# Block attention: 64-row head operands with shift and mask rows, filled by DMA, and an even first-pass stream

## The chip, the cores and the metric

The kernel runs on one core of one Trainium2 chip. The metric is the device time of one execution in microseconds (us), lower is better. Three timed executions of the kernel before gave 1613.99, 1619.00 and 1619.61 us, so the median is 1619.0 us.

## The reference, cut to what matters

Four blocks follow each other on `x` of shape (2, 1024, 128): rotary attention, a mixture of 8 experts, block attention and a channel mix. Only the third is touched. It has 16 heads of 8 channels and this core:

```python
q = (hidden_states @ Wq.T + bq).reshape(B, S, NUM_HEADS, HEAD_DIM)
k = (hidden_states @ Wk.T + bk).reshape(B, S, NUM_HEADS, HEAD_DIM)
v = (hidden_states @ Wv.T + bv).reshape(B, S, NUM_HEADS, HEAD_DIM)
scores = jnp.einsum('bihd,bjhd->bhij', q, k) / scale
blk = jnp.arange(S) // WINDOW                  # WINDOW = 32
allowed = blk[:, None] >= blk[None, :]
scores = jnp.where(allowed, scores, jnp.zeros((), scores.dtype))
probs = jax.nn.softmax(scores, axis=-1)
ctx = jnp.einsum('bhij,bjhd->bihd', probs, v).reshape(B, S, H)
return ctx @ Wo.T + bo
```

A score that is not allowed is 0, not minus infinity, so later keys still count in the softmax, each with weight exp(0 - maximum).

## The kernel before

`block_attention` first projects `q` and `k` (the part that ends in lines 1000 to 1032). Each head gets 32 rows of `q_all` and of `k_all`: its 8 channels four times over, split in high and low parts for fp32r matmuls. Then the main part works on 8 groups (2 batches times 4 groups of 4 heads), each in two passes.

The first pass finds the maximum of each query's row. A fill step `i` of a group does two heads (`query_scores`, lines 1160 to 1178): a matmul with 32 rows of queries as weights and up to 512 keys moving (L1173), and a matmul with 3 mask rows (L1176) on the 128x128 block on the diagonal. The result lies in one of three PSUM banks `score_ps`, and VectorE takes its maximum (`row_max`, L1300) and frees the bank. A group has 20 fill steps, listed in `KINDS`, that is 40 banks. From the maxima VectorE makes rows of shifts, TensorE transposes them (`shift_transposes`, L1129, L1130) and ScalarE keeps them in `shift` and `later` (L1258, L1259).

The second pass goes by key tiles of 128 keys. A group has 24 steps: `block_of` gives the half of the queries, the key tile `kt` and the pair of heads `hp`. `key_scores` (L1140) multiplies keys (weights) by up to 512 queries for two heads, `key_shifts` (L1151, L1156) adds shift and mask rows in matmuls of 5 or 2 rows over the same columns, and ScalarE takes the exponential of both heads into `probs_T` (`exps`, L1268). After every second step `values` (L1190) multiplies 9 columns of `v_den` by `probs_T` for four heads; for the key tiles 0 to 3 of either half it adds the later keys (`suffix`, L1196). `keep_out` (L1274) copies the sum, `turn` (L1206) transposes it, `divide` (L1327, L1332) finishes it. After the last group of a batch come `transpose_attn` (L1214), `project` (L1222) and the additions to the residual.

The order is written out by hand: for `m` in 0 to 9 and `i` in 0 to 23 the step `(m, i)` runs the second pass of group `m - 1` and, for `i` below 20, a fill step of group `m`. The heads of the two lie in different row quarters of TensorE. The program order in a step is `key_scores`, `query_scores(i, 0)`, `key_shifts`, `query_scores(i, 1)`, and then `values` if `i` is odd:

```python
def fill_of(i, x):
    return KINDS[i // 2], 2 * (1 - i % 2) + x
...
pe.wait_ge(bank_free, n - 2)      # query_scores: one of three banks must be free
```

`m = 0` has only fill steps, `m = 8` only the second pass of the last group. SyncE issues nothing in the main part. GpSimd clears `zeros` there; in the projection part it clears and copies constants from `fixed` (lines 919 to 937), and VectorE waits for that (`zeroed`, 2) before line 1032.

Of the kernel before, what the change touches and what calls it, by code (L numbers as in the profile page):

```python
# [10 lines left out]
P = 128  # L11
B, N, D = 2, 1024, 128
T = B * N // P
TB = N // P
# [8 lines left out]
HG = 4  # L23
EPS = 1e-5
NEVER = 2.0 ** 99
BLOCK_CONSTS = 1307
# [829 lines left out]
def block_attention(nc, core, consts, Wq, bq, Wk, bk, Wv, bv, Wo, bo):  # L856
# [6 lines left out]
    with ExitStack() as st:  # L863
# [6 lines left out]
        shift_keys = sb("shift_keys", [P, P], F32R)  # L870
        mask_q, mask_k = sb("mask_q", [P, P], F32R), sb("mask_k", [P, P], F32R)
        fixed = sb("fixed", [P, BLOCK_CONSTS])
        later_cap = fixed[:, 776:792].rearrange("p (t h) -> p t h", t=4)
        own_block = fixed[:, 792:920].rearrange("p (i t r) -> p i t r", i=2, t=4)
        shift_rows = [sb(f"shift_rows{i}", [P, 4, HG, 32]) for i in range(2)]
# [3 lines left out]
        with ExitStack() as st2:  # L879
# [37 lines left out]
            with nc.Block() as block:  # L917
                @block.gpsimd
                def _(pool):
# [9 lines left out]
                    for i in range(2):  # L929
                        below = fixed[:, 920:923].rearrange("p (t h r) -> p t h r", t=1, h=1).broadcast_to([P, 4, HG, 3])  # L930
                        nc.gpsimd.tensor_copy(shift_rows[i][:, :, :, 2:5], below)
# [3 lines left out]
                    nc.gpsimd.tensor_copy(shift_keys[:], fixed[:, 923:1051])  # L935
                    nc.gpsimd.tensor_copy(mask_q[:], fixed[:, 1051:1179])
                    nc.gpsimd.tensor_copy(mask_k[:], fixed[:, 1179:1307]).then_inc(zeroed, 1)
# [98 lines left out]
        STEPS = 24  # L1036
        KINDS = ((0, 0, 1), (1, 0, 2), (2, 0, 3), (3, 0, 4), (4, 0, 4), (5, 0, 4), (6, 0, 4), (6, 4, 7), (7, 0, 4), (7, 4, 8))
        FILL_STEPS = 2 * len(KINDS)
        Z_STEP, T_HALF0, T_HALF1 = 9, 16, 4
        TURN0, TURN1, KEEP0, KEEP1 = 13, 4, 11, 2  # L1040
        shift = [sb(f"shift{i}", [P, N], F32R) for i in range(2)]
        later = [sb(f"later{i}", [P, 2, P]) for i in range(2)]
        lowest = sb("lowest", [P, 12, HG])
        capped = sb("capped", [P, 4, HG])
        probs_T = [sb(f"probs_T{i}", [P, HG, 512]) for i in range(3)]
        out_kept = [sb(f"out_kept{i}", [P, 512]) for i in range(2)]
        rden = [sb(f"rden{i}", [P, 4, HG]) for i in range(2)]
        attn = sb("attn", [P, TB, H1, DH1])
# [5 lines left out]
        out_ps = ps("out", [P, 512])  # L1054
        bank_filled, bank_free = sem("bank_filled"), sem("bank_free")
        pair_filled, pair_free = sem("pair_filled"), sem("pair_free")
        capped_ready, halves_ready, shift_ready = sem("capped_ready"), sem("halves_ready"), sem("shift_ready")
        pv_done, out_copied, rden_ready, main_cleared = (sem(n) for n in ("pv_done", "out_copied", "rden_ready", "main_cleared"))

        def filling(m, i):  # L1060

            return m < GROUPS and i < FILL_STEPS

        def summing(m):

            return 1 <= m <= GROUPS

        def turned(m, i):

            if i == TURN0 and 1 <= m <= GROUPS:  # L1070
                return m - 1, 0
            if i == TURN1 and 2 <= m <= GROUPS + 1:
                return m - 2, 1
            return None

        def projected(m, i, after):

            got = turned(m, i - after)
            return got if got and got[0] % G == G - 1 else None

        bank, pair = {}, {}
        for m in range(GROUPS + 2):
            for i in range(STEPS):
                if (i == T_HALF1 and summing(m)) or (i == T_HALF0 and m < GROUPS):
                    pair["shift", m, i] = len(pair)
                if summing(m):
                    pair["scores", m, i] = len(pair)
                if filling(m, i):
                    for x in range(2):
                        bank["fill", m, i, x] = len(bank)  # L1090
                if turned(m, i):
                    bank["turn", m, i] = len(bank)
                if projected(m, i, 3):
                    bank["attn_T", m, i] = len(bank)
                if projected(m, i, 6):
                    bank["project", m, i] = len(bank)

        def fill_of(i, x):

            return KINDS[i // 2], 2 * (1 - i % 2) + x  # L1100

        def block_of(i):

            half, r = (0, i) if i < 8 else (1, i - 8)
            return half, r // 2, r % 2
# [5 lines left out]
        def keyed(m):  # L1111

            return (m - 1) * 12

        with nc.Block() as block:
            @block.gpsimd
            def _(pool):
                nc.gpsimd.memset(zeros[:], 0.0).then_inc(main_cleared, 1)

            @block.tensor  # L1120
            def _(pe):
                def shift_transposes(half, m, i):
                    n = pair["shift", m, i]
                    if n >= 2:
                        pe.wait_ge(pair_free, n - 1)
                    pe.wait_ge(halves_ready, 2 * (m - half) + half + 1)
# [5 lines left out]
                def key_scores(m, i):  # L1132
                    half, kt, hp = block_of(i)
                    b, g = (m - 1) // G, (m - 1) % G
                    lo, hi = columns(half, kt)
                    n = pair["scores", m, i]
                    pe.wait_ge(pair_free, max(n - 1, pair["shift", m if half else m - 1, T_HALF1 if half else T_HALF0] + 1))
                    for x in range(2):
                        rows = slice(64 * hp + 32 * x, 64 * hp + 32 * x + 32)
                        nc.tensor.matmul(score_T_ps[n % 2][:, x, 0:hi - lo], k_all[rows, g, b * N + kt * P:b * N + kt * P + P],  # L1140
                                         q_all[rows, g, b * N + lo:b * N + hi], start=True, stop=False)

                def key_shifts(m, i):
                    half, kt, hp = block_of(i)
                    lo, hi = columns(half, kt)
                    n = pair["scores", m, i]
                    off = P if lo == P * kt else 0
                    if off:
                        for x in range(2):
                            rows = slice(64 * hp + 32 * x, 64 * hp + 32 * x + 5)  # L1150
                            ins = nc.tensor.matmul(score_T_ps[n % 2][:, x, 0:P], shift_keys[rows, :], shift[(m - 1) % 2][rows, lo:lo + P],  # L1151
                                                   start=False, stop=hi - lo == P)
                    if hi - lo > off:
                        for x in range(2):
                            rows = slice(64 * hp + 32 * x, 64 * hp + 32 * x + 2)
                            ins = nc.tensor.matmul(score_T_ps[n % 2][:, x, off:hi - lo], shift_keys[rows, :], shift[(m - 1) % 2][rows, lo + off:hi],  # L1156
                                                   start=False, stop=True)
                    ins.then_inc(pair_filled, 1)

                def query_scores(m, i, x):  # L1160
                    (t, lo, hi), h = fill_of(i, x)
                    b, g = m // G, m % G
                    n = bank["fill", m, i, x]
# [5 lines left out]
                    rows = slice(32 * h, 32 * h + 32)  # L1169
                    for t, lo, hi, at in parts:  # L1170
                        width = (hi - lo) * P
                        own = hi == t + 1
                        ins = nc.tensor.matmul(score_ps[n % 3][:, at:at + width], q_all[rows, g, b * N + t * P:b * N + t * P + P],  # L1173
# [382 lines left out]
```

## Time and profile before

| | us |
|---|---|
| median of three timed executions | 1619.0 |
| the profiled execution, its own time | 1619.23 |
| its span, first to last instruction | 1617.3 |
| main part of block attention in it, first to last fill or second-pass step | 1171.1 to 1575.7 |

The profiled execution is an ordinary one: its time lies within those of the timed three. Times in rows are from the start of the span. "PE" is TensorE's matmuls, "PEld" its weight loads, "DVE" VectorE, "ACT" ScalarE, "POOL" GpSimd, "SP" SyncE. PEclk is the clock that TensorE was granted, as a share of 2.4 GHz; it has two levels, 1.0 and 0.5 (1.2 GHz), and a value between is a mean of the two over the stretch. In a timeline row the first number is the start, the second how long the merged run of instructions took, and `x8` how many they are; a release by another engine stands in brackets.

### The profile page before, as it was taken

What the parts mean: (1) busy time and instruction counts of PE and PEld (TensorE: products, weight loads), DVE (VectorE), ACT (ScalarE), POOL (GpSimd) and SP (SyncE); (2) the same over time, 40 slices, a digit from 0 to 9 for tenths busy, and PEclk for the clock granted to TensorE, in tenths of its full rate; (3) what the DMA queues carried; (4) which work ended last, traced back from release to release, by engine and by line L of the source; (5) the groups of instructions that cost most, each with busy time, mean ns of one, the idle gap of its engine ahead of it and who ended that gap; (6) DMA issues with size and microseconds to landing.
All of it is one profiled execution on the core that took longest, in us unless ns stands there. A gap on an engine that the chain in (4) does not pass through costs nothing. (4 is left out here: it accounts for less than half of the span.)

```text
span 1617.3 us, 26411 instructions
## 1 busy us (share of the span) xinstructions
PE 1429.3 (88%) x9399; PEld 967.4 (60%) x9400; DVE 830.4 (51%) x1461; ACT 892.0 (55%) x1582; POOL 280.9 (17%) x206
## 2 busy tenths in 40 slices
PE   3499999999999999999999962954899999999995
PEld 2377777777777777777777741642465455555443
DVE  5355445555555555555545532535775564464406
ACT  2277777777777777777777720311624444353443
POOL 3233113312321232123212303023000000000000
PEclk9799999999999999999999975985955565585557
DMA  4542344234423442344234423111000000000001
GB/s 129 127 111 73 78 110 110 71 78 110 110 69 75 109 116 56 82 110 117 59 83 110 111 90 126 45 46 40 1 1 1 1 1 1 1 1 1 1 1 31
DMA packets 53477, 104.93 MB, mean 65 GB/s; under 512 B 9010, under 2 KB 30004, under 8 KB 53300
## 3 DMA queue, kind: packets, MB, share of 16 engines
q1 hardware_dynamic: 52004, 100.59, 25.2%
q0 software_dynamic: 1424, 3.67, 0.8%
q8 instruction: 32, 0.52, 0.1%
q14 instruction: 17, 0.14, 0.0%
HBM read 18.70 MB, written 5.31 MB: 15 GB/s over the span
## 5 line engine op out<-in xcount | busy, mean ns | idle before, releaser
L507 DVE TENSOR_REDUCE a_negmax<-a_score 128x1 f32<-128x1024 f32 x257 | 314.5, 1224 | 327.4 <-PE a_score L371 327.4
L468 ACT ACTIVATE a_probs_T<-a_tr 128x512 f32<-128x512 f32 x514 | 279.2, 597 | 214.4 <-PE a_tr L377 210.9
L474 ACT ACTIVATE a_probs<-a_score,a_negmax 128x1024 f32<-128x1024 f32 x256 | 287.9, 1124 | 28.6 <-DVE a_negmax L507 28.5
L377 PE MATMUL a_tr<-ident,a_probs 128*128 128x128 f32 x2056 | 267.2, 273 | 0.4 <-ACT a_probs_T L468 0.4
L377 PEld LDWEIGHTS a_tr<-ident,a_probs 128*128 128x128 f32 x2056 | 239.5, 140 | 38.0 <-issue 5.7
L432 PE MATMUL a_out<-a_probs_T,a_v 128*64 128x256 f32 x2096 | 255.1, 385 | 0.0
L1300 DVE TENSOR_REDUCE a_lowest<-a_score 128x1 f32<-128x512 f32 (+3 forms) x320 | 183.8, 630 | 131.8 <-PE a_score L1176 81.1
L1268 ACT ACTIVATE a_probs_T<-a_score_T 128x1024 f32<-128x1024 f32 (+1 forms) x192 | 149.0, 809 | 171.5 <-PE a_score_T L1156 150.8
L432 PEld LDWEIGHTS a_out<-a_probs_T,a_v 128*64 128x64 f32 x2096 | 138.8, 136 | 96.8 <-issue 38.0
L1173 PE MATMUL a_score<-a_k_all,a_q_all 32*128 32x512 f32 (+3 forms) x384 | 164.3, 611 | 5.3 <-DVE a_lowest L1300 5.0
L331 POOL TENSOR_TENSOR a_rden<-a_rden_col,a_ones 128x256 f32<-128x256 f32 x65 | 68.4, 1052 | 557.3 <-DVE a_rden_col L530 557.3
L1190 PE MATMUL a_out<-a_probs_T,a_v_den 128*9 128x512 f32 (+3 forms) x768 | 132.2, 779 | 4.5 <-ACT a_out_kept L1274 4.3
L1140 PE MATMUL a_score_T<-a_q_all,a_k_all 32*128 32x512 f32 (+3 forms) x384 | 114.4, 614 | 0.8 <-ACT a_probs_T L1268 0.6
L1173 PEld LDWEIGHTS a_score<-a_k_all,a_q_all 32*128 32x128 f32 x384 | 85.1, 276 | 28.8 <-DVE a_lowest L1300 23.9
L1156 PE MATMUL a_score_T<-a_shift,a_shift_keys 2*128 2x512 f32 (+3 forms) x320 | 85.2, 530 | 0.0
L371 PE MATMUL a_score<-a_k_stack0ah,a_q_stack0a 128*128 128x512 f32 x130 | 58.8, 452 | 28.5 <-DMA a_k_stack0bl<-a_k_lo 28.5
L1140 PEld LDWEIGHTS a_score_T<-a_q_all,a_k_all 32*128 32x128 f32 x384 | 56.9, 277 | 39.3 <-ACT a_probs_T L1268 19.3
L1196 PEld LDWEIGHTS a_out<-a_later,a_suffix 16*128 16x128 f32 x128 | 30.0, 289 | 82.6 <-issue 82.6
L523 DVE TENSOR_TENSOR a_attn_T<-a_out,a_rden_b 128x256 f32<-128x256 f32 x66 | 28.0, 424 | 86.9 <-PE a_out L432 86.9
L147 PE MATMUL n_tp<-ident,n_xn 128*128 128x128 f32 x48 | 12.1, 422 | 64.0 <-DVE n_xn L134 64.0
L357 PE MATMUL a_misc<-a_xn_cur,a_w_cur 128*128 128x512 f32 x128 | 65.5, 594 | 0.0
L371 PE MATMUL a_score<-a_k_stack1ah,a_q_stack1a 128*128 128x512 f32 x128 | 57.4, 448 | 6.7 <-DMA a_k_stack1bl<-a_k_lo 6.7
(235 smaller groups left out, 2203.8 us busy)
## 6 DMA issues: line engine op xcount, KB each, us to landing
a_q_rot<-a_q_raw SPq DMA_DIRECT2D x68, 128.0 KB, 2.3
a_k_rot<-a_k_raw SPq DMA_DIRECT2D x68, 128.0 KB, 2.3
a_xn_cur<-normed_T SPq DMA_DIRECT2D x17, 512.0 KB, 3.2
a_k_stack0ah<-a_k_hi SPq DMA_DIRECT2D x18, 256.0 KB, 3.3
a_k_stack0al<-a_k_lo SPq DMA_DIRECT2D x18, 256.0 KB, 4.7
a_k_stack0bh<-a_k_hi SPq DMA_DIRECT2D x18, 256.0 KB, 5.0
a_k_stack0bl<-a_k_lo SPq DMA_DIRECT2D x18, 256.0 KB, 4.7
a_k_stack1ah<-a_k_hi SPq DMA_DIRECT2D x16, 256.0 KB, 3.3
```

Source lines behind the costliest of these rows:

```text
L371: last = nc.tensor.matmul(score_ps[s % 2][:, cols], q_stack[par][h][:, tile * P:tile * P + P], k_stack[par][h][part][:, cols], start=part ...
L377: last = nc.tensor.transpose(tr_ps[k // 4][:, k % 4 * P:k % 4 * P + P], probs[s % 4][:, k * P:k * P + P], core.ident[:])
L432: ins = nc.tensor.matmul(out_ps[64 * h:64 * h + 64, 0:256], v[par if s >= 5 else 1 - par][:, k, 64 * h:64 * h + 64], probs_T[grp][:, h, k, ...
L468: nc.scalar.activation(probs_T[(s - 1) // 4 % 2][:, h, 4 * i:4 * i + 4, tile % 2 * P:tile % 2 * P + P], tr_ps[i][:].rearrange("p (k q) -> ...
L474: nc.scalar.activation(probs[s % 4][:], score_ps[s % 2][:], ACT.Exp, bias=negmax[:, s:s + 1], accum_out=den[:, s:s + 1]).then_inc(probs_re ...
L507: nc.vector.tensor_reduce(negmax[:, s:s + 1], score_ps[s % 2][:], axis=AX.X, op=ALU.max, negate=True)\
L1140: nc.tensor.matmul(score_T_ps[n % 2][:, x, 0:hi - lo], k_all[rows, g, b * N + kt * P:b * N + kt * P + P], q_all[rows, g, b * N + lo:b * N ...
L1156: ins = nc.tensor.matmul(score_T_ps[n % 2][:, x, off:hi - lo], shift_keys[rows, :], shift[(m - 1) % 2][rows, lo + off:hi], start=False, st ...
L1173: ins = nc.tensor.matmul(score_ps[n % 3][:, at:at + width], q_all[rows, g, b * N + t * P:b * N + t * P + P], k_all[rows, g, b * N + lo * P ...
L1190: ins = nc.tensor.matmul(out_ps[32 * h:32 * h + DH1 + 1, lo - 512 * half:512], v_den[:, b, kt, g * HG + h, :], probs_T[n % 3][:, h, 0:hi - ...
L1268: nc.scalar.activation(probs_T[k % 3][:, 2 * hp:2 * hp + 2, 0:hi - lo], score_T_ps[n % 2][:, :, 0:hi - lo], ACT.Exp).then_inc(pair_free, 1)
L1300: nc.vector.tensor_reduce(to, src, axis=AX.X, op=ALU.max, negate=True).then_inc(bank_free, 1)
```

## The change

Each head of a group gets 64 rows of its own in new operands: `q_still` (queries as weights, first pass), `q_moving` (queries moving, second pass) and `k_cur` (keys, both passes). Rows 0 to 31 are the head's rows of `q_all` or `k_all`, rows 32 and 33 the two parts of the shift (ones in `k_cur`), rows 34 to 36 the mask. The mask rows and ones are laid out once by GpSimd, in 14 copies of 128x1024 in the projection part, where three copies of 128x128 and two of 128x48 go. The head's rows come by DMA on SP's queue, 4 copies of 128 KB each for `q_still`, `q_moving` and `k_cur` and for every group; the shift rows come by 4 small DMAs for each half group (`place_shift`).

With this a block of the second pass is one matmul pass of 34 rows (37 on the diagonal) in place of a pass of 32 and one of 2 or 5 rows, and a block of the first pass needs no mask matmul of its own. Two heads now fill the 128 rows, where four row quarters were used.

The loop runs over `j` from -1: `j = -1` does 25 fill steps (`LEAD`), then every step of the second pass is followed by 20/24 of a fill step, until all 160 are done; the last 30 steps have none. The fill step that falls out is that of every sixth step (`j % 6 == 0`). Shift transposes stand ahead of fill step 12 of a group and 4 of the next. `out_kept` and `attn` lie in the space of `core.xT`, and `lowest` has two buffers.

```diff
+        STEPS, FILLS = 24, 20
+        LEAD, LAG = 25, 5
+        TURN0, TURN1, KEEP0, KEEP1 = 13, 28, 10, 26
...
+        def fills_by(j):
+
+            return min(GROUPS * FILLS + LAG, LEAD + (j + 1) * FILLS // STEPS)
+
+        def fills_at(j):
+
+            return range(0, LEAD) if j < 0 else range(fills_by(j - 1), fills_by(j))
...
+                def place_shift(m, half):
+                    sp.wait_ge(shift_kept, 2 * m + half + 1)
+                    for h in range(HG):
+                        sp.dma_start(q_moving[m % 2][h // 2][64 * (h % 2) + 32:64 * (h % 2) + 34, 512 * half:512 * half + 512].bitcast(F32),
+                                     shift[half][32 * h:32 * h + 2, :].bitcast(F32)).then_inc(shift_loaded[half], 16)
+
+                load_still(0)
+                load_keys(0)
+                load_still(1)
+                load_keys(1)
+                load_moving(0)
+                for m in range(GROUPS):
+                    if m >= 2:
+                        sp.wait_ge(pair_filled, pair["scores", (m - 1) * STEPS - 1] + 1)
+                    if m >= 1:
+                        load_moving(m)
+                        if m + 1 < GROUPS:
+                            load_keys(m + 1)
+                    place_shift(m, 0)
+                    if m + 2 < GROUPS:
+                        sp.wait_ge(bank_filled, bank["fill", (m + 1) * FILLS - 1, 1] + 1)
+                        load_still(m + 2)
+                    place_shift(m, 1)
...
+                def key_scores(j):
+                    m, half, kt, hp = block_of(j)
                     lo, hi = columns(half, kt)
...
+                    if j % STEPS == 0:
+                        pe.wait_ge(moving_loaded[m % 2], LOADED * (m // 2 + 1))
+                        pe.wait_ge(k_loaded[m % 3], LOADED * (m // 3 + 1))
+                    if j % STEPS in (0, 8):
+                        pe.wait_ge(shift_loaded[half], LOADED * (m + 1))
+                    pe.wait_ge(pair_free, n - 1)
                     off = P if lo == P * kt else 0
                     if off:
                         for x in range(2):
...
+                            rows = slice(64 * x, 64 * x + 37)
+                            ins = nc.tensor.matmul(score_T_ps[n % 2][:, x, 0:P], k_cur[m % 3][hp][rows, kt * P:kt * P + P],
+                                                   q_moving[m % 2][hp][rows, lo:lo + P], start=True, stop=True)
                     if hi - lo > off:
                         for x in range(2):
...
+                            rows = slice(64 * x, 64 * x + 34)
+                            ins = nc.tensor.matmul(score_T_ps[n % 2][:, x, off:hi - lo], k_cur[m % 3][hp][rows, kt * P:kt * P + P],
+                                                   q_moving[m % 2][hp][rows, lo + off:hi], start=True, stop=True)
...
+                    if f % FILLS == 0 and x == 0:
+                        pe.wait_ge(still_loaded[m % 2], LOADED * (m // 2 + 1))
+                        pe.wait_ge(k_loaded[m % 3], LOADED * (m // 3 + 1))
...
-                            query_scores(m, i, 0)
...
-                            key_shifts(m, i)
...
-                            query_scores(m, i, 1)
...
+                for j in JOBS:
+                    if live(j):
+                        key_scores(j)
+                    for f in fills_at(j):
+                        if shift_at(f):
+                            shift_transposes(*shift_at(f))
+                        if f < GROUPS * FILLS:
+                            query_scores(f, 0)
+                            query_scores(f, 1)
+                    if j % 2 == 1 and live(j - 3):
+                        values((j - 3) // STEPS, (j - 3) % STEPS // 2)
```

## Rows read from the trace of the kernel before

**Rows 1.** The page: the granted clock in 40 slices of the span.

```profile
PEclk9799999999999999999999975985955565585557
```

**Rows 2.** Stretches: length, busy of PE, PEld, DVE, ACT, POOL; clock; DMA share.

```profile
1171.10:1195.50 24.40, 22.80 (x86) 16.07 (x85) 21.21 (x42) 2.16 (x3) 0.00 (x0) 0.50 0.00 0
1195.50:1245.30 49.80, 48.93 (x322) 26.51 (x320) 26.95 (x59) 20.61 (x29) 0.00 (x0) 0.50 0.00 1
...
1294.70:1338.50 43.80, 42.59 (x337) 21.81 (x333) 25.00 (x53) 20.95 (x31) 0.00 (x0) 0.64 0.00 1
...
1392.00:1435.90 43.90, 42.92 (x349) 24.00 (x345) 26.72 (x55) 20.95 (x30) 0.00 (x0) 0.68 0.00 1
1435.90:1481.30 45.40, 43.97 (x337) 22.38 (x333) 25.00 (x53) 20.77 (x30) 0.00 (x0) 0.62 0.00 1
...
1531.50:1575.70 44.20, 42.29 (x259) 20.02 (x257) 2.48 (x6) 19.75 (x28) 0.00 (x0) 0.50 0.00 1
```

**Rows 3.** Timeline, steps 16 and 17 of the second group, clock 0.5.

```profile
1283.20 0.79 PE L1140 MATMUL a_score_T<-a_q_all,a_k_all 32*128 32x512 f32 x2
1283.21 0.81 PE L1173 MATMUL a_score<-a_k_all,a_q_all 32*128 32x512 f32 x2
...
1283.80 0.30 PE L1151 MATMUL a_score_T<-a_shift,a_shift_keys 5*128 5x128 f32 x2
...
1283.90 0.62 PE L1156 MATMUL a_score_T<-a_shift,a_shift_keys 2*128 2x384 f32 x2
1284.05 2.48 DVE L1300 TENSOR_REDUCE a_lowest<-a_score 128x1 f32<-128x512 f32 x4 [3.99 <-PE a_score L1173]
...
1284.80 0.79 PE L1173 MATMUL a_score<-a_k_all,a_q_all 32*128 32x512 f32 x1
...
1285.52 1.90 PE L1190 MATMUL a_out<-a_probs_T,a_v_den 128*9 128x512 f32 x8
```

**Rows 4.** Timeline around the suffix matmuls of the first group, clock 0.5.

```profile
1220.64 0.58 PE L1196 MATMUL a_out<-a_later,a_suffix 16*128 16x128 f32 x1
1220.65 0.79 PE L1140 MATMUL a_score_T<-a_q_all,a_k_all 32*128 32x512 f32 x1
...
1221.09 0.77 PE L1140 MATMUL a_score_T<-a_q_all,a_k_all 32*128 32x512 f32 x1
...
1223.38 1.90 PE L1190 MATMUL a_out<-a_probs_T,a_v_den 128*9 128x512 f32 x8
1225.21 0.79 PE L1196 MATMUL a_out<-a_later,a_suffix 16*128 16x128 f32 x2
1225.93 1.11 PE L1206 MATMUL a_score<-ident,a_out_kept 128*128 128x128 f32 x4
```

**Rows 5.** Timeline, the start of the main part.

```profile
1168.55 0.53 POOL L1118 MEMSET a_zeros<- 128x512 f32 x1 [45.79 <-SPq L1115]
1171.13 0.50 PE L1173 MATMUL a_score<-a_k_all,a_q_all 32*128 32x128 f32 x3
```

**Rows 6.** DMA issues: KB each, median us to landing.

```profile
a_q_rot<-a_q_raw SPq DMA_DIRECT2D x68, 128.0 KB, 2.3
a_q_stack0b<-a_q_lo SPq DMA_DIRECT2D x9, 256.0 KB, 4.9
```

**Rows 7.** Groups by form on GpSimd (busy us, mean ns); a timeline row of DVE.

```profile
L338 POOL TENSOR_TENSOR a_q_lo<-a_q_raw,a_q_hi 128x1024 fp32r<-128x1024 f32 x17 | 41.2, 2426 | 53.9 <-DVE a_q_hi L516 53.9
L935 POOL CAST a_shift_keys<-a_fixed 128x128 fp32r<-128x128 f32 x1 | 0.3, 288 | 0.0
1148.66 0.87 DVE L1032 TENSOR_TENSOR a_suffix<-a1p_b_ps,a_fixed 128x128 f32<-128x128 f32 x4
```

**Rows 8.** A stretch at each level of the clock, and the projection before one rise.

```profile
1225.00:1245.00 20.00, 20.00 (x131) 10.23 (x127) 8.27 (x19) 7.92 (x12) 0.00 (x0) 0.50 0.00 1
1419.80:1436.80 17.00, 16.36 (x176) 8.48 (x173) 10.82 (x24) 9.98 (x15) 0.00 (x0) 1.00 0.00 1
1415.31 2.08 PE L1222 MATMUL a_score<-a_wo_T,a_attn_T 128*128 128x128 f32 x8
```

More of the change, by code:

```diff
@@ new lines, in columns_at, with turned, projected @@
+        def columns_at(f):
+            if f % FILLS == 8 and f < GROUPS * FILLS:
+                return f // FILLS, 0
+            if f % FILLS == 0 and f >= FILLS:
+                return f // FILLS - 1, 1
+            return None
+        def turned(j):
+            for half, at in enumerate((TURN0, TURN1)):
+                if (j - at) % STEPS == 0 and live(j - at):
+                    return (j - at) // STEPS, half
+            return None
+        def projected(j, after):
+            got = turned(j - after)
@@ L1079, in projected @@
             return got if got and got[0] % G == G - 1 else None
         bank, pair = {}, {}
[L1082 to L1096, printed above, removed]
@@ L1098, in fill_of @@
-        def fill_of(i, x):
-            return KINDS[i // 2], 2 * (1 - i % 2) + x
-        def block_of(i):
+        JOBS = range(-1, GROUPS * STEPS + 12)
+        for j in JOBS:
+            if live(j):
+                pair["scores", j] = len(pair)
+            for f in fills_at(j):
+                if shift_at(f):
+                    pair[("shift",) + shift_at(f)] = len(pair)
+                for x in range(2):
+                    if f < GROUPS * FILLS:
+                        bank["fill", f, x] = len(bank)
+            if turned(j):
+                bank[("turn",) + turned(j)] = len(bank)
+            if projected(j, 3):
+                bank[("attn_T",) + projected(j, 3)] = len(bank)
+            if projected(j, 6):
+                bank[("project",) + projected(j, 6)] = len(bank)
@@ L1130, in shift_transposes @@
                     nc.tensor.transpose(to[:, 1, 0:P], later_rows[half][:].rearrange("p t r -> p (t r)"), core.ident[:]).then_inc(pair_filled, 1)
-                def key_scores(m, i):
-                    half, kt, hp = block_of(i)
-                    b, g = (m - 1) // G, (m - 1) % G
+                def key_scores(j):
+                    m, half, kt, hp = block_of(j)
                     lo, hi = columns(half, kt)
[L1136 to L1146, printed above, removed]
+                    n = pair["scores", j]
+                    if j % STEPS == 0:
[4 more added lines that the diff above has]
+                    pe.wait_ge(pair_free, n - 1)
                     off = P if lo == P * kt else 0
@@ L1261, in exps @@
-                def exps(m, i):
-                    half, kt, hp = block_of(i)
+                    if m:
+                        act.wait_ge(shift_loaded[half], LOADED * m)
+                    nc.scalar.activation(shift[half][:], score_T_ps[n % 2][:, 0, :], ACT.Copy).then_inc(shift_kept, 1)
+                    nc.scalar.activation(later[m % 2][:, half, :], score_T_ps[n % 2][:, 1, 0:P], ACT.Exp).then_inc(pair_free, 1)
+                def exps(j):
+                    m, half, kt, hp = block_of(j)
@@ L1263, in exps @@
                     lo, hi = columns(half, kt)
[L1264 removed]
+                    n, k = pair["scores", j], j // 2
                     act.wait_ge(pair_filled, n + 1)
@@ L1312, in shift_columns @@
+                        nc.vector.tensor_scalar(capped[:], low[:, 0:4, :], 0.0, None, ALU.min).then_inc(capped_ready, 1)
                         dve.wait_ge(capped_ready, 3 * m + 1)
                     if m >= 1:
-                        dve.wait_ge(pair_filled, pair["shift", m - 1 + half, T_HALF1 if half else T_HALF0] + 1)
+                        dve.wait_ge(pair_filled, pair["shift", m - 1, half] + 1)
                     nc.vector.tensor_copy(shift_rows[half][:, :, :, 0].bitcast(F32R), capped[:]).then_inc(shift_ready, 1)
```

309 lines of the change are left out of this document (152 added, 157 removed).

## The prediction

> **What bounds the kernel now.** I read the page's clock line first. Up to about 1170 us TensorE has mostly the full clock, and from there it is mostly at 0.5, that is 1.2 GHz [rows 1]. The stretches come next. The main part of block attention goes from 1171.1 to 1575.7 us, a quarter of the span. A group of 24 steps takes 49.8 us in which PE is busy for 48.9, DVE for 27.0 and ACT for 20.6; two more like it took as long [rows 2]. So TensorE sets the pace, at half its clock. Three groups have the full clock for a part of their time (means of 0.64, 0.68 and 0.62) and take 43.8, 43.9 and 45.4 us [rows 2]. Only the span of that main part can move: I found nothing of the change outside it but GpSimd's copies.
>
> What fills a group is read from timelines. In steps 16 and 17 two key blocks (L1140) and two query blocks (L1173) start within 0.01 us of each other, since their heads lie in four row quarters; the shift blocks of 128 and 384 columns follow the key blocks on the same rows [rows 3]. 128 columns take 0.10 us there (1283.80 to 1283.90), so 512 take 0.43, and 0.17 go into the first start. The second pair of steps' last query block starts at 1284.80 because one of three banks has to be free: the first block ends after 0.8 us, DVE takes 0.69 for its maximum (2.48 us for four, 0.62 apiece in a row), and from there it is 0.72 to `values`. The score part of this step pair is 1285.52 - 1283.20 = 2.32 us, and it is this chain over a bank that makes it so, not the 1.9 us of columns.
>
> **The cost of a group, part by part.** `values` of 512 columns takes 1.83 us (1223.38 to 1225.21) [rows 4], 1.71 of it columns in four passes; a group has nine times 512 in 12 calls, 9 x 1.71 + 12 x 0.12 = 16.8 us. The suffix blocks delay one of the key blocks by 0.44 (1220.65 to 1221.09) [rows 4], eight times, 3.5. Four sets of transposes at 1.1 to 1.3 (1.11 for four) [rows 4] make 4.8. So 25.1 us of 49.8 are not touched and the 12 score parts have 24.7.
>
> *After*, a score part holds key and query blocks one behind the other, since a head now has 64 rows and two heads fill the array, but no shift or mask pass. At full width the four blocks are 4 x 0.43 = 1.71 us. That is what the half clock's key and shift passes took already: fusing them saves no columns in a step in which query blocks ran beside them for nothing. The bank chain gets longer by a key block, 2.32 + 0.43 = 2.75. The even stream gives 20 fill steps to 24: eight step pairs have two of them and four have one. (1) Five pairs with two run uninterrupted: 2.75 twice, 2.6 twice and 2.0 once, as their key, first and last query blocks are narrower (0.11 us per 128 columns each, and the maximum of 256 columns is shorter too): 12.7. (2) In three of them, steps 4, 9 and 23, transposes now stand between the two fill steps, and the wait for a bank passes under them; columns alone count, 1.7, 2.2 and 1.4 = 5.3. (3) Four with one fill step have no bank to wait for: 0.17 + three blocks + 0.1, that is 1.45 at most, 4.9 for the four. Together 22.9 against 24.7, so -1.8 us a group, for seven groups -12.6.
>
> The last 30 steps have no fill steps. In the last group before, 44.2 us without any query block [rows 2], the shift pass is bare: 24 blocks with 9216 columns, 18 x 0.43 = 7.7 us, all of it on PE's path, and it goes: -7.7. Six steps of the group ahead lose their query blocks: 2.0 - 0.7, 1.4 - 0.5 and 1.1 - 0.9, -2.4. In return 25 instead of 20 fill steps stand ahead of the first second-pass step. Twenty took 24.4 us there with DVE busy for 21.2 [rows 2], so DVE bounds them; the five are ten maxima, six of them under 512 columns: at 0.62 for 512 some 4.7 (6.1 by the mean of the twenty): +4.7.
>
> **New waits.** The first fill step waits for eight copies of 128 KB. One lands in 2.3 us, the last of a burst of 256 KB copies in 4.9 [rows 6]; they can be issued when GpSimd's clearing starts, at 1168.55, and the first matmul comes at 1171.13 now [rows 5]. That is 1168.6 + (4.9 to 7) - 1171.1 = 2.4 to 4.5 late: +3.5. Queued behind it on PE is all the rest, so it counts in full. Later copies have time: `load_keys` and `load_moving` follow the end of a group and serve steps 18 or more steps on, 35 us at this pace; the shift rows of the second half are made at step 23 and wanted at step 8, 15 us on, for two hops of 2.3. The SP queue holds nothing else. If the clock is high these are 9 us, still enough: 0. GpSimd's 14 copies of 128x1024 lie between 0.95 us (from 0.29 for 128 columns) and 2.4 (its two-operand form) each [rows 7], 13 to 34 us from 1122; the VectorE instruction that waits for them comes at 1148.66, so they hide by the low price, and cost 7 by the high one. A copy is nearer the low: 0. ACT loses nothing and gains nothing: 20.6 busy in 48.
>
> Weight loads: a head's key weights are loaded as before for a block, hidden behind the block ahead (no gap between the 128 and 384 columns) [rows 3]; the shift's and mask's loads go. Cost 0, between 0 and 0.17 a block if a half array did not hide them; nothing in the rows points to that.
>
> **Sum**, against the profiled execution's own 1619.2 us (the median is 1619.0, so they stand for each other): 3.5 + 4.7 - 12.6 - 2.4 - 7.7 = -14.5, that is **1605 us**, with the full clock coming and going as it does now (its three visits are worth 3 x 49.8 - 133.1 = 16 us, and stay in the sum). Own range 1592 to 1615.
>
> **Rivals.** *A, the clock stays up.* The engine was busy for 20.00 of 20 us and had 0.5, and it had 1.0 for 17 us in which it was busy for 16.4; the rise came behind a projection (L1222) on all 128 rows [rows 8]. So being busy is not enough here, and what runs in the array must matter. After the change no matmul of 2, 3 or 5 rows is left, and score blocks take up both halves of the array; on the other side 34 rows of 64 do work. The pace at 1.0: the group of 43.9 at mean 0.68 has 15.8 us of it, its 28.1 at half are 0.56 of a group, so the rest makes 36 a group; the one at 0.64 gives 33. Say 33 after the change. One group at 48, six at 33, the last at 25, in place of 354: -83, **1522**; DVE's 25 us busy a group is the floor, 1474. For it: three rises already. Against it: two of three fell within 14 us.
> The Trainium skill ("TensorE: Matmul & The Clock Gate", Part 1) says that the throttled state is the default and that activity releases it. By busy time alone that does not hold in these rows; if denser use is activity, it is this rival, with 1522.
>
> *B, the suffix no longer overlaps: slower.* A suffix block uses 16 rows of a quarter, and the key and query blocks in other quarters start 0.01 us behind it; ahead of a 128-row transpose the same two pieces take 0.72 (1225.21 to 1225.93) [rows 4]. If blocks of 64 rows have to wait like the transposes, each of 64 suffixes costs 0.72 - 0.44 = 0.28 more, and 0.17 for a start-up that no longer lies beside it: 18 to 29 us, **1623 to 1634**. It decides from 0.23 us each (no gain) and 0.35 (clearly slower).
> The Trainium skill ("TensorEngine Tiling (Array Packing)", Key Properties) states that changing the tiling mode drains TensorE. It gives no time; it speaks for this rival, as 16-row and 64-row blocks are of different modes and 16-row and 32-row blocks were not.
>
> *C, the stream does not do what it says.* With DVE's bank chain and the serial heads a group stays at 49.8; only the ends move: **1617**.
>
> **Chances.** Forecast 0.42, A 0.28, B 0.17, C 0.13. A measurement tells 0.5% (8 us) from no change: below 1611 is faster, above 1627 slower. Faster is A and three quarters of the forecast, 0.60; slower is B at its upper price (0.10) and what I priced at nothing (0.06), 0.16; the rest is 0.24. The range has to reach into A and B: 1500 to 1632; the forecast's own stands above.
>
> **What would show it.** The first score matmul some 3 us later, behind the SP queue; the first second-pass step 8 us later; groups of 48 us at clock 0.5 with score parts of 2.75, 1.45; a last group of 36.5. Clock at 1.0 for most of 1220 to 1560 is A; key blocks starting 0.7 us behind the suffix is B. PE waits for SP's shift copies, or weight loads with PE idle beside them, would make the sum wrong in a way I give little chance.

## The result, and the profile after

The changed kernel takes 1662.1 us, median of 4 runs (1657.3 to 1674.8), against 1617.5 us of the kernel before (1614.0 to 1619.6). The ratio is 1.029 with a 95% interval of 1.022 to 1.036: slower, where I forecast 1605. The profiled execution is the slowest of the four, with 1674.8 us and a span of 1673.0, so the rows below are to be compared with the 1619.2 us of before: 55.6 us. Its mean granted clock is 0.813 and that of the other three 0.822 to 0.825, so it shows the loss at its largest; by the medians it is 44.6 us. Executions over 1.5% above the fastest of the same kernel are left out of medians and ratios below, which touches one, in experiment 1.

The clock line of the page answers to [rows 1], and the stretches, with the columns of [rows 2], to those of before:

```profile
PEclk9799999999999999999999859959555555555557
```

```profile
1181.10:1211.70 30.60, 29.75 (x110) 22.35 (x112) 27.28 (x57) 2.51 (x4) 0.00 (x0) 0.50 0.29 65
1264.40:1318.00 53.60, 53.30 (x278) 29.02 (x274) 25.32 (x54) 21.09 (x30) 0.00 (x0) 0.50 0.13 31
1371.60:1428.00 56.40, 56.09 (x290) 31.00 (x286) 26.74 (x56) 21.09 (x30) 0.00 (x0) 0.50 0.13 29
1484.20:1537.80 53.60, 53.30 (x278) 29.01 (x274) 25.31 (x54) 21.09 (x30) 0.00 (x0) 0.50 0.09 21
1588.30:1632.00 43.70, 41.70 (x212) 18.69 (x212) 2.48 (x6) 19.32 (x26) 0.00 (x0) 0.50 0.00 1
```

A plain group takes 53.6 us (49.8 before, [rows 2]; 48 forecast), and TensorE is busy for 53.3 of them. There are three of these; the first takes 52.7, the two that hold a projection 56.4 and 56.2, and the one that runs out of fill steps 50.5. The clock never leaves 0.5 in any of them. The three visits to the full clock of [rows 2] are gone. The last group takes 43.7 us, where it took 44.2.

The start of the main part: the timelines of GpSimd and of TensorE, which answer to [rows 5], and the first key block of the second pass.

```profile
1117.08 0.09 POOL L922 MEMSET a1p_ones<- 1x4 f32 x1 [15.46 <-POOLq L81]
...
1174.24 0.53 POOL L1192 MEMSET a_zeros<- 128x512 f32 x1 [33.31 <-POOLq L919]
```

```profile
1181.16 1.86 PE L1249 MATMUL a_score<-a_k_cur,a_q_still 37*128 37x128 f32 x8 [4.27 <-DMA a_k_cur<-a_k_all]
...
1211.73 0.42 PE L1220 MATMUL a_score_T<-a_q_moving,a_k_cur 37*128 37x128 f32 x2
```

The clearing starts 5.7 us later than in [rows 5] (1168.55). GpSimd's first instruction of block attention is already 0.8 us late, at 1117.08; in the kernel before it came at 1116.32:

```profile
1116.32 0.09 POOL L920 MEMSET a1p_ones<- 1x4 f32 x1 [15.45 <-SPq L917]
```

So 4.9 of the 5.7 us arise between this instruction and the clearing. From the clearing the first score matmul comes after 6.9 us instead of 2.6, since it waits 4.3 us for a copy by DMA. From it to the first key block it is 30.6 us instead of 24.3. Together 16.2 us.

Where the 4.9 us arose is seen in the grouped instructions of VectorE from 1125 to 1160 us, before and then after (mean ns of one behind the comma):

```profile
L1018 DVE SCALAR_TENSOR_TENSOR a_q_all<-a1p_full,a1p_part,a1p_high 128x512 fp32r<-128x512 f32 x16 | 11.9, 750 | 3.1 <-ACT a1p_high L994 2.5
L1015 DVE TENSOR_SCALAR a1p_high<-a1p_full,a1p_part 128x512 fp32r<-128x512 f32 x12 | 5.8, 480 | 4.6 <-ACT a1p_full L989 4.6
```

```profile
L1022 DVE SCALAR_TENSOR_TENSOR a_q_all<-a1p_full,a1p_part,a1p_high 128x512 fp32r<-128x512 f32 x16 | 14.9, 940 | 1.2 <-ACT a1p_high L998 0.9
L1019 DVE TENSOR_SCALAR a1p_high<-a1p_full,a1p_part 128x512 fp32r<-128x512 f32 x9 | 6.7, 739 | 6.1 <-ACT a1p_full L993 6.1
```

The means rose from 0.75 to 0.94 us and from 0.48 to 0.74, though the stretch also holds instructions that ran after GpSimd's casts, which end at 1141. One with a cast beside it, and one behind the last cast:

```profile
1134.72 1.26 DVE L1019 TENSOR_SCALAR a1p_high<-a1p_full,a1p_part 128x512 fp32r<-128x512 f32 x1
...
1142.66 0.47 DVE L1019 TENSOR_SCALAR a1p_high<-a1p_full,a1p_part 128x512 fp32r<-128x512 f32 x1
```

Now a pair of steps with two fill steps, from TensorE's timeline in a group at 0.5, then a suffix of the same group:

```profile
1295.63 0.79 PE L1225 MATMUL a_score_T<-a_q_moving,a_k_cur 34*128 34x512 f32 x2
1296.22 0.62 PE L1245 MATMUL a_score<-a_k_cur,a_q_still 34*128 34x512 f32 x2
1296.65 0.63 PE L1225 MATMUL a_score_T<-a_q_moving,a_k_cur 34*128 34x512 f32 x2
1297.08 1.35 PE L1245 MATMUL a_score<-a_k_cur,a_q_still 34*128 34x512 f32 x2
1298.35 1.89 PE L1262 MATMUL a_out<-a_probs_T,a_v_den 128*9 128x512 f32 x8
...
1300.18 0.79 PE L1268 MATMUL a_out<-a_later,a_suffix 16*128 16x128 f32 x2
1300.90 0.47 PE L1220 MATMUL a_score_T<-a_q_moving,a_k_cur 37*128 37x128 f32 x2
1301.17 0.63 PE L1225 MATMUL a_score_T<-a_q_moving,a_k_cur 34*128 34x384 f32 x2
1301.60 0.52 PE L1245 MATMUL a_score<-a_k_cur,a_q_still 34*128 34x384 f32 x2
```

The uninterrupted pair takes 2.72 us (1295.63 to 1298.35), as forecast (2.75). But the key blocks behind the suffix start 0.72 us after it (1300.18 to 1300.90), and not 0.01 us for one and 0.44 for the other as in [rows 4]. That is the mechanism of rival B.

The four terms of the half-clock group, each read from the start of its first block to the start of what follows, for all blocks from 1264.43 to 1318.04: `values` 16.7 us (forecast 16.8), transposes 4.6 (4.8), eight suffixes at 0.72 5.8 (3.5), score parts 26.5 (22.9). In all 53.6, where 48.0 were forecast.

### The profile page after: what moved, and what is told of

It is laid out like the page before. It is cut to its first block and busy times, and to the rows that moved or that the text cites. A ratio compares the mean times of both kernels' runs of the same rounds, so it can differ in the third digit from the quotient of the medians.

```text
span 1673.0 us, 25732 instructions
## 1 busy us (share of the span) xinstructions
PE 1482.8 (89%) x8951; PEld 1001.6 (60%) x8952; DVE 836.5 (50%) x1461; ACT 893.5 (53%) x1582; POOL 298.3 (18%) x215
## 5 line engine op out<-in xcount | busy, mean ns | idle before, releaser
L1262 PE MATMUL a_out<-a_probs_T,a_v_den 128*9 128x512 f32 (+3 forms) x768 | 140.6, 826 | 1.8 <-ACT normed_T L1337 1.8
L1245 PE MATMUL a_score<-a_k_cur,a_q_still 34*128 34x512 f32 (+3 forms) x320 | 118.1, 580 | 0.9 <-DVE a_lowest L1361 0.7
L1225 PE MATMUL a_score_T<-a_q_moving,a_k_cur 34*128 34x512 f32 (+3 forms) x320 | 92.1, 596 | 0.0
L1245 PEld LDWEIGHTS a_score<-a_k_cur,a_q_still 34*128 34x128 f32 x320 | 68.1, 315 | 20.6 <-DVE a_lowest L1361 14.3
L1220 PEld LDWEIGHTS a_score_T<-a_q_moving,a_k_cur 37*128 37x128 f32 x256 | 38.6, 304 | 40.8 <-issue 23.5
L371 PE MATMUL a_score<-a_k_stack0bh,a_q_stack0b 128*128 128x512 f32 x128 | 61.1, 477 | 0.0
```

The lines of the kernel that those rows point to most:

```text
L371: last = nc.tensor.matmul(score_ps[s % 2][:, cols], q_stack[par][h][:, tile * P:tile * P + P], k_stack[par][h][part][:, cols], start=part ...
L1245: ins = nc.tensor.matmul(score_ps[n % 3][:, at:at + rest], q_still[m % 2][hp][rows, t * P:t * P + P], k_cur[m % 3][hp][rows, lo * P:lo * P ...
L1262: ins = nc.tensor.matmul(out_ps[32 * h:32 * h + DH1 + 1, lo - 512 * half:512], v_den[:, b, kt, g * HG + h, :], probs_T[n % 3][:, h, 0:hi - ...
```

## Experiments

The theory after this result had four parts: the suffix blocks drain TensorE now; the clock stays low because of what runs in the array; GpSimd's casts slow VectorE; and the rest is the order or the operands. The rivals are in the expectations. Each ratio is against the kernel before on the same chip; the changed kernel itself was not run again there, so differences to its 1662.1 us are between chips.

**1 and 2. The suffix left out**, in the kernel before and in the changed one.

```diff
-                        ins = nc.tensor.matmul(out_ps[:, kt * P:kt * P + P], suffix[rows, b, half, ...], later[...][rows, half, :], ...)
```

> The kernel before without its 64 suffix blocks (the output lacks their contribution). In the trace of before a suffix delays one key block by 0.44 us and a transpose by 0.72. Theory (the suffix no longer overlaps once score blocks have 64 rows): here it costs 5 x 0.44 + 3 x 0.72 = 4.4 us a group at the low clock, 28 to 35 us in all, so 1585 to 1590 against 1617 before. Rival (the suffix costs the same in both kernels and the loss of the change lies elsewhere): the saving here equals that of the same edit to the changed kernel.

> The changed kernel without its 64 suffix blocks (the output lacks their contribution). In its trace every one of them holds the next block up by 0.72 us. Theory: 64 x 0.72 = 46 us less, 1616 against 1662, which is 12 to 18 us more than the same edit gives in the kernel before. Rival: the same saving in both kernels, about 30 us, and 1632 here.

Before without suffixes: 1555.3 us, ratio 0.962 (0.955 to 0.969). The changed kernel without them: 1598.9, ratio 0.989 (0.987 to 0.991). The first saving is 61 us (from 1616.4) and the second 63. The two don't differ beyond the intervals, and both are well over what either expectation gave, 28 to 35 and 30 to 46 us. Only at a clock of 0.5 can the price of the blocks be read. A group of the changed kernel without suffixes:

```profile
1258.60:1306.40 47.80, 47.49 (x262) 25.08 (x258) 25.33 (x54) 21.09 (x30) 0.00 (x0) 0.50 0.15 34
```

53.6 - 47.8 = 5.8 us, eight times 0.72: the suffix's own price in the changed kernel. Both kernels gained more than their suffixes cost, because the clock rose: the mean granted clock of the whole span was 0.872 instead of 0.836, and 0.845 instead of 0.813 to 0.825. So this pair of totals neither shows nor refutes B, which the timelines do show; it said that the clock answers to these blocks.

**3. All 64 rows driven.** The same instructions, with rows 37 to 63 of each head, which are zeros, given to every score block. The three mask rows act on all blocks then, not on the diagonal ones alone, so scores off the diagonal are other ones.

```diff
-                            rows = slice(64 * x, 64 * x + 34)
+                            rows = slice(64 * x, 64 * x + 64)
```

> The changed kernel with all 64 rows of a head given to every score block (the rows past 37 are zeros; the mask rows act on every block, so the scores of blocks off the diagonal are other ones). The count of instructions and of columns is the same. Theory (it is how many rows are driven that decides whether the clock is raised): the granted clock is 1.0 for most of the main part, groups go from 53.6 us towards 33 to 37, and the kernel takes 1510 to 1560. Rival (the clock doesn't look at rows): 0.5 throughout as in the changed kernel, 1662 within 0.5 per cent.

1537.4 us, ratio 0.954 (0.948 to 0.960). The page's clock line and a group:

```profile
PEclk9699999999999999999999998589577589999976
```

```profile
1289.40:1323.40 34.00, 31.45 (x278) 17.67 (x274) 25.19 (x54) 20.72 (x30) 0.00 (x0) 1.00 0.21 48
```

278 matmuls and 274 weight loads, as in the changed kernel's group at 1264.40, the same columns, and TensorE has 2.4 GHz instead of 1.2: 34.0 us instead of 53.6. From the second group on every group of the second pass with fill steps has a granted clock of 1.00; the first has a mean of 0.66 and takes 42.8. Apart from the count of rows, only the values differ that the mask rows add off the diagonal, and experiment 7 has the right values and the same clock. So the clock rose with the rows driven, of which 27 in each head hold zeros. The rival, that it doesn't look at rows, is out.

**4. The stream alone**, with 32-row operands, separate shift and mask blocks, and none of the copies and casts. **5. The operands alone**, with the old order:

```diff
-        LEAD, LAG = 25, 5
+        LEAD = FILLS
...
-            return min(GROUPS * FILLS + LAG, LEAD + (j + 1) * FILLS // STEPS)
+            return min(GROUPS * FILLS + 5, LEAD + (j + 1) // STEPS * FILLS + min((j + 1) % STEPS, FILLS))
```

> The even stream and the longer lead of the change with the operands of the kernel before: 32 rows a head, separate shift and mask blocks, no copies by DMA, none of GpSimd's fourteen copies. Theory (the operands make the change slow and the stream is nearly neutral): the first second-pass step 5 us later than before, groups of 48 to 51 us at the low clock, 1612 to 1632. Rival (the stream makes it slow, since the score blocks of a one-fill step have nothing beside them): groups of 53, 1645 to 1660.

> The changed kernel with the order of the kernel before: 20 query blocks' steps ahead of the second pass and one in each of the first 20 of a group's 24 steps. The 64-row operands, their copies and GpSimd's casts stay. Theory (the stream costs 30 us by itself, as stream_32rows shows, and adds to what the operands cost): first second-pass step 6 us earlier than in the changed kernel, groups of 51 to 52 us instead of 53.6, 1628 to 1642. Rival (with 64-row operands the stream does what it is for, and the loss of stream_32rows belongs to 32-row operands alone): 1655 to 1675.

The stream alone: 1649.7 us, ratio 1.021 (1.019 to 1.022). The operands alone: 1663.0, ratio 1.034 (1.026 to 1.042). One half-clock group of each:

```profile
1252.30:1304.20 51.90, 50.25 (x334) 27.41 (x330) 25.54 (x53) 21.20 (x30) 0.00 (x0) 0.50 0.00 1
```

```profile
1257.20:1312.90 55.70, 55.66 (x278) 30.18 (x274) 25.16 (x53) 21.28 (x30) 0.00 (x0) 0.50 0.13 30
```

Both theories were wrong: that the stream is nearly neutral (1612 to 1632 for the stream alone), and that the costs add (1628 to 1642 for the operands alone). Both times lie where the rival had them, though the stream's groups are not the 53 us of its rival. With 32 rows a head the stream makes a group longer, 49.8 to 51.9 us; with 64 it makes it shorter, 55.7 to 53.6. The longer lead costs some 7 us with either operands (31.0 us instead of 24.3 from the first score matmul to the second pass with 32 rows, 30.6 instead of 23.6 with 64), and of the visits to the full clock the operands alone keep one (a group of 46.0 us at a mean of 0.72) and the stream alone hardly any. So each half of the change is slower by itself, and the stream pays 2.1 us a group of it back only beside 64-row operands. A reason that fits, not tested: the old order puts query blocks next to key blocks of other row quarters, which overlap, and the even one doesn't keep this; with 64-row operands nothing of it is there to lose.

**6. Without GpSimd's casts.** ScalarE makes the extra rows once (two casts of 32 rows), and SP copies them 26 times.

```diff
-                            nc.gpsimd.tensor_copy(k_cur[i][hp][:].rearrange("p (t k) -> p t k", t=TB), extra(1))
...
+                    nc.scalar.activation(q_still[0][0][32:64, :], extra_f32[32:64, :], ACT.Copy)
...
+                                        sp.dma_start(to[i][hp][64 * x + 32:64 * x + 64, :].bitcast(F32), src.bitcast(F32)).then_inc(extra_loaded, 16)
```

> The changed kernel, with the shift and mask rows of the operands put in place by ScalarE's two casts of 32 rows and 26 copies by DMA in place of GpSimd's 14 casts of 128x1024. Theory (GpSimd's casts slow the VectorE instructions beside them and so the projections): the main part starts at 1168.5 to 1169.5 us instead of 1174.2 and the kernel takes 1656. Rival (the later start has another cause, such as the clock of the projections): it stays at 1174 and 1662.

1647.9 us, ratio 1.019 (1.016 to 1.022). The clearing that opens the main part, and the first of VectorE's two groups ahead of it:

```profile
1166.86 0.52 POOL L1204 MEMSET a_zeros<- 128x512 f32 x1 [46.89 <-POOLq L922]
```

```profile
L1034 DVE SCALAR_TENSOR_TENSOR a_q_all<-a1p_full,a1p_part,a1p_high 128x512 fp32r<-128x512 f32 x16 | 11.9, 750 | 2.7 <-ACT a1p_high L1010 2.2
```

The mean is 0.75 us again and the main part begins 7.4 us earlier. Of these, 2.2 lie ahead of GpSimd's first instruction of the block, which comes at 1114.89. From that instruction to the clearing it is 51.9 to 52.3 us in all ten traces without the 14 casts and 56.8 to 57.2 in all four with them, so the casts cost some 5 us. The median fell by 14 us, more than twice what was expected; in its trace two groups have a visit to the full clock (45.6 and 45.5 us), which the changed kernel's profiled execution lacks.

**7 and 8. Mask rows of their own for each diagonal block**, on top of experiment 6, so that 58 rows carry data, one matmul of 64 rows is enough for every block, and the scores are those of the reference; then **the suffix as one 128-row block** of 512 columns per half.

```diff
-                            rows = slice(64 * x, 64 * x + 37)
...
+                        rows = slice(64 * x, 64 * x + 64)
+                        ins = nc.tensor.matmul(score_T_ps[n % 2][:, x, 0:hi - lo], k_cur[m % 3][hp][rows, kt * P:kt * P + P],
+                                               q_moving[m % 2][hp][rows, lo:hi], start=True, stop=True)
```

```diff
-                    if kt < 4:
...
+                    if kt == 0:
+                        ins = nc.tensor.matmul(out_ps[:], suffix[:, b, half, g * HG:(g + 1) * HG, :].rearrange("p h r -> p (h r)"),
+                                               later[m % 2][half][:], start=False, stop=False, skip_group_check=True)
```

> The kernel of the run above with mask rows of their own for each of the eight diagonal blocks (24 rows), so that every score block takes all 64 rows of a head and needs no split at the diagonal; it computes what the reference does. Theory (driven rows raise the clock): as after_rows64 less the 5 us of the casts, 1525 to 1540, granted clock over 0.9. Rival (in after_rows64 it was not the rows but the masks' effect on other instructions, or zeros in the rows don't count as driven): 1656.

> rows58 with the suffix as one block of 128 rows and 512 columns per half (block-diagonal operand, four exps of 16 rows in place of one) instead of four blocks of 16 rows and 128 columns. At the full clock a suffix costs some 0.6 us (0.72 at half, of which 0.43 is columns) and there are eight a group; two blocks of 512 columns cost 0.86 each. Theory (draining the array is what the small blocks cost): 1 to 3 us less a group, 1512 to 1525. Rival (the drain is hidden at full clock or the bound is elsewhere by then): no change against rows58.

1525.1 us, ratio 0.941 (0.936 to 0.945), and 1513.1, ratio 0.935 (0.933 to 0.938). The second one's clock line and a group:

```profile
PEclk9699999999999999999999999569759599999986
```

```profile
1272.80:1305.80 33.00, 30.15 (x218) 13.13 (x214) 24.99 (x54) 22.23 (x37) 0.00 (x0) 1.00 0.22 49
```

**9. The same suffix in the kernel before**, with what belongs to it as in experiment 8: ScalarE's exponential in four parts of 16 rows, and four clearings by GpSimd.

> The kernel before with the suffix as one block of 128 rows and 512 columns per half. At the low clock 4.4 us a group go and 3.4 come, 8 us less in all. Theory (few driven rows hold the clock down, and the 64 suffix blocks of 16 rows were part of that, as before_no_suffix with a mean clock of 0.872 suggests): more time at the full clock, 1565 to 1595. Rival (the clock of before_no_suffix came from the time without the blocks, not from the rows): 1605 to 1612.

1561.8 us, ratio 0.965 (0.963 to 0.968), a little below the range that I gave.

```profile
PEclk9699999999999999999999996597595778887786
```

```profile
1238.10:1279.90 41.80, 38.85 (x322) 18.64 (x318) 25.14 (x53) 22.57 (x37) 0.00 (x0) 0.76 0.00 1
```

The mean clock of this group is 0.76, and those of the seven groups with fill steps are 0.70 to 0.87, where by the stretches of [rows 2] four of the seven had 0.50 or 0.51. At half the clock the edit is worth about 1 us a group by columns and waits, an estimate that the expectation has; so of the 57 us some 49 are the clock's. This edit does not isolate the rows: it also takes away small blocks and what they hold up, and without any suffix block (experiment 1) the clock had risen to 0.872 as well, with 0.895 here.

**10 to 12. What is left at the full clock**: the old order, the first 20 copies issued in the projection stage, and both.

```diff
+                        sp.wait_ge(stack_ready, steps)
...
+                                sp.dma_start(bufs[hp][64 * x:64 * x + 32, :].bitcast(F32), src[32 * h:32 * h + 32, g, 0:N].bitcast(F32)).then_inc(loaded_sem, 16)
```

> rows58_suffix128 with the order of the kernel before in place of the even stream. Theory (the longer lead costs and an even stream returns nothing): the second pass starts 6 us earlier, groups as long as they are (33.0 us), 1505 to 1509. Rival (at the full clock VectorE's maxima are the next bound, and the even stream is what keeps them fed): groups of 34 to 35, 1515 to 1525.

> rows58_suffix128 with the first 20 copies of heads issued in the projection stage, as soon as their columns are written. Theory: the 4.1 us wait for them at the start goes, 1508 to 1510. Rival (the copies then slow the projections, or their issue waits behind the 26 copies of mask rows on the same queue): 1513 or later.

> Both edits of the two runs above. If they add: 1499 to 1505; if the order decides at the full clock by VectorE, as the rival of best_order20 has it: 1510 to 1521.

| kernel | us | ratio, interval | second pass starts | group |
| --- | --- | --- | --- | --- |
| rows58_suffix128 | 1513.1 | 0.935, 0.933 to 0.938 | 1205.7 | 33.0 |
| with the old order | 1517.9 | 0.940, 0.936 to 0.945 | 1198.9 | 34.1 |
| with early copies | 1510.2 | 0.936, 0.931 to 0.940 | 1199.5 | 33.0 |
| both | 1520.5 | 0.940, 0.934 to 0.946 | 1195.0 | 34.1, the last two 37.1 at a mean clock of 0.91 |

At the full clock the even stream gives back 1.1 us a group, some 8 in seven, and the lead takes 6.8 of it again; I had expected the old order to win there (1505 to 1509) and both edits to add (1499 to 1505), and both times lie where the rivals had them. Whether VectorE's maxima are the reason, as those rivals say, is not shown. With early copies the first score matmul no longer waits:

```profile
1167.65 2.07 PE L1298 MATMUL a_out<-a_zeros 128*128 128x512 f32 x2 [4.96 <-POOL a_zeros L1208]
1169.66 11.19 PE L1255 MATMUL a_score<-a_k_cur,a_q_still 64*128 64x128 f32 x29
```

The ratios of these four don't separate; each beats both kernels of the case.

## Why the prediction was wrong

By its own terms, in the profiled executions (us):

| term | forecast | measured |
| --- | --- | --- |
| earlier in the span, no term | 0 | +0.8 |
| GpSimd's casts | 0 | +4.9 |
| wait for the first copies | +3.5 | +4.3 |
| five more fill steps ahead | +4.7 | +6.2 |
| seven groups | -12.6 - 2.4 | +40.5 |
| last group, up to its transposes | -7.7 | -1.1 |
| sum | -14.5 | +55.6 |

Four steps of the working failed: the suffix counted as untouched, the sizes of the score parts, the shift pass of the last group counted as bare, and GpSimd's casts at nothing. Besides, the sum kept the three visits to the full clock.

**The groups.** Against the forecast they lost 55.5 us. 16 are the three visits to the full clock, which I kept in the sum. The rest is 5.6 us in each half-clock group (53.6 - 48.0), times seven 39.

**The suffix (3.5 kept as "not touched") failed**: rival B had the mechanism, at its lower price of 0.28 us each; the start-up of its upper price is found in the score parts below. 0.72 us for each of eight suffixes instead of 0.44 makes 2.3 a group, 16 in seven. Not all of it is the change's: in the kernel before three suffixes a group already stood ahead of transposes at 0.72 us (at 1203.58, 1225.21 and 1230.99 in the first group), so its suffixes cost some 4.4 and not 3.5, and the change added some 1.4. B alone does not account for the result: its highest time was 1634 us, 28 below the median. I had the 0.72 in [rows 4], from a suffix ahead of a 128-row transpose, and gave B 0.17. The Trainium skill ("TensorEngine Tiling (Array Packing)", Key Properties) states that a change of the tiling mode drains TensorE. This trace agrees: 0.72 where the next block has 64 rows, 0.01 to 0.44 in [rows 4] where it has 32.

**The score parts failed by size**: 26.5 instead of 22.9, the largest part of the miss in a group. Part (1), five uninterrupted pairs, came out at 13.6 for 12.7 (2.72, 2.62, 2.73, 2.83, 2.68): the chain over a bank was right. Part (2) was the worst: "columns alone count" gave 5.3, and it was 7.1. One of the three, between `values`, a suffix and transposes:

```profile
1271.93 0.47 PE L1220 MATMUL a_score_T<-a_q_moving,a_k_cur 37*128 37x128 f32 x2
1272.20 0.42 PE L1225 MATMUL a_score_T<-a_q_moving,a_k_cur 34*128 34x128 f32 x2
1272.42 0.74 PE L1245 MATMUL a_score<-a_k_cur,a_q_still 34*128 34x512 f32 x2
1273.09 1.11 PE L1277 MATMUL a_score<-ident,normed_T 128*128 128x128 f32 x4
1274.13 0.47 PE L1220 MATMUL a_score_T<-a_q_moving,a_k_cur 37*128 37x128 f32 x2
```

256 key and 512 query columns are 0.64 us at 0.107 per 128, and the part takes 1.16 (1271.93 to 1273.09): 0.17 more in the first block, 0.11 more in the second (128 columns in 0.22), and 0.24 between the last column and the transposes. A score part that transposes break in two pays the first and the last of these twice. In part (3), pairs with one fill step, my ceiling of 1.45 was none: 1.69, 1.16, 1.47 and 1.48, 5.8 for 4.9.

**The last group (-7.7) failed by logic.** I counted the shift pass there as bare on TensorE's path, and the key pass as unchanged. Timelines of a pair of steps in the last group, before and then after (of the eight matmuls of `values` the window holds four):

```profile
1558.74 0.81 PE L1140 MATMUL a_score_T<-a_q_all,a_k_all 32*128 32x512 f32 x4
1559.34 0.64 PE L1156 MATMUL a_score_T<-a_shift,a_shift_keys 2*128 2x512 f32 x4
1559.90 1.04 PE L1190 MATMUL a_out<-a_probs_T,a_v_den 128*9 128x512 f32 x4
```

```profile
1609.34 1.22 PE L1225 MATMUL a_score_T<-a_q_moving,a_k_cur 34*128 34x512 f32 x4
1610.49 1.04 PE L1262 MATMUL a_out<-a_probs_T,a_v_den 128*9 128x512 f32 x4
```

Before, the two steps' four key blocks run together in the four row quarters, then the four shift blocks: 1.16 us. After, four fused blocks fill the array two at a time: 1.15 us. Fusing halves the passes and halves what runs side by side. I had said so for the pairs with fill steps and forgot it here.

**GpSimd's casts (0) failed**, for 4.9 us. Their length was as I took it (19 us for fourteen), and nobody waited for GpSimd, as I said. The cost lay on VectorE, whose instructions slowed down beside them.

**Weight loads (0) failed a little.** Behind the narrow block on the diagonal, 384 columns take 0.43 us instead of 0.32 (1301.17 to 1301.60 above). Without the split (experiment 7, in the first three pairs of steps of its second pass, at the same clock) it is 1.75, 5.16 and 4.62 us from each pair's first block to the next pair's, for 1.96, 5.27 and 4.84: 0.1 to 0.2 a pair with a diagonal block. That these are the loads of two heads' weights behind a short block is argued, not shown.

**What held:** the wait for the first copies (4.3 for 3.5), copies later on (no wait of TensorE for a DMA after 1211.7), the price of a group at the full clock (34.0 us in experiment 3, 33 in rival A).

**Rival A had the mechanism and the wrong sign.** "What runs in the array must matter" is right, and the counter-argument in it, 34 rows of 64, weighed more than I gave it: two heads' blocks drive 68 rows, and with 128 driven by the same blocks (experiment 3) the clock was up. Why the visits of the kernel before went is not shown by this: the stream alone, with its 32-row operands, had hardly any either, and the operands alone kept one. Its sum has a slip: by [rows 2] and the forecast's own terms the eight groups were to take 380.2 - 22.7 = 357.5 us, not 354, which gives 1518 and not 1522. The Trainium skill ("TensorE: Matmul & The Clock Gate", Part 1) lets activity release the throttle; here TensorE was busy for 53.3 of 53.6 us at 0.50 and for 31.5 of 34.0 at 1.00, so its busy time does not tell the two apart; the rows driven do. What exactly is counted, rows, elements or both, the runs do not tell apart.

## What to carry to other kernels

Where TensorE sets the pace at half its clock, look first at how many rows its matmuls drive: padding operands with rows of zeros, or turning small-row blocks into one of 128 rows, was worth more here (57 to 125 us, some 8 of the 57 by columns and waits) than all that was saved in columns. When heads or tiles are fused into taller operands, count what ran side by side before, and what a small block holds up at each change of row tiling: 0.72 us at the low clock for one of 16 rows and 128 columns, its own columns included. And work put on an idle GpSimd is not free while VectorE is on the path.

## What the runs showed of the hardware that I had not expected

Rows of zeros raised the granted clock from 0.50 to 1.00 with the same counts of instructions and columns (53.6 to 34.0 us a group). A suffix block of 16 rows and 128 columns holds a following 64-row block for 0.72 us and a 32-row block of another quarter for 0.01. GpSimd's casts of 128x1024 stretched VectorE's 128x512 instructions beside them by a quarter to a half in the mean (0.75 to 0.94 us, 0.48 to 0.74), and single ones to 1.26 us.
